# Self-attention: the value products of a unit's four chunks gathered into one visit of TensorE

## The reference, cut to what matters

```python
q = (x @ Wq.T + bq).reshape(b, l, h, hd).transpose(0, 2, 1, 3)   # b=16, l=64, h=32, hd=16
k = (x @ Wk.T + bk) ...
v = (x @ Wv.T + bv) ...
scores = jnp.einsum('bhqd,bhkd->bhqk', q, k) / math.sqrt(hd)
scores = jnp.where(causal, scores, -jnp.inf)
att = jax.nn.softmax(scores, axis=-1)
out = jnp.einsum('bhqk,bhkd->bhqd', att, v)                        # the value products
return out.transpose(0, 2, 1, 3).reshape(b, l, d) @ Wo.T + bo
```

## Time and profile before

| | us |
|---|---|
| median of three runs | 704.95 |
| the profiled execution, whole | 706.06 |
| its span, first to last instruction | 704.2 |
| TensorE busy in the span | 694.8 |
| the 110 us from 538.5 to 648.5 (the 16 steps): TensorE busy | 110.0 |
| the same: VectorE busy | 95.0 |
| the same: GpSimd busy | 89.7 |
| the same: ScalarE busy | 74.9 |

### The profile page before, as it was taken

One profiled execution on the slowest core, in us unless ns is written; L12 is line 12 of the kernel. 1 busy time (PEld: TensorE's weight loads), 2 busy tenths in 40 slices (PEclk: granted clock), 3 DMA queues, 4 the chain that ended last, 5 costly groups with the idle time before them and its releaser, 6 DMA issues.

```text
span 704.2 us, 12879 instructions
## 1 busy us (share of the span) xinstructions
PE 694.8 (99%) x4841; PEld 564.0 (80%) x4841; DVE 516.4 (73%) x815; ACT 373.0 (53%) x560; POOL 471.6 (67%) x360
## 2 busy tenths in 40 slices
PE   8999999899999999999999999999999999999998
PEld 6887888688888888888888888887888888887886
DVE  5566988967767767857758758748668888899734
ACT  6356665634743743753653653654246777665220
POOL 2698155877777778778777877844525799985630
PEclk9999999999999999999999999999999999999999
DMA  7645613140400311310310312200300101011003
GB/s 263 221 150 176 172 46 106 75 164 17 135 31 18 132 35 38 106 45 30 104 45 30 104 45 65 87 16 2 104 2 1 46 31 33 2 47 46 16 1 119
DMA packets 25736, 51.08 MB, mean 73 GB/s; under 512 B 2400, under 2 KB 10720, under 8 KB 25696
## 3 DMA queue, kind: packets, MB, share of 16 engines
q1 hardware_dynamic: 25696, 50.53, 21.8%
HBM read 40.04 MB, written 10.49 MB: 72 GB/s over the span
## 4 chain that ended last, share of the span: by engine, by line
PE 83%; DVE 5%; POOL 4%; DMA 3%; issue 2%; ACT 2%; SPq 1%; DVEq 0%; POOLq 0%; ACTq 0%
PE pj L1625 12%; PE pv L1712 10%; PE pj L1712 10%; PE pj L1816 9%; PE tp L1625 8%; PE sc L1681 4%; PE tp L1712 4%; PE pj L2000 3%; PE pv L1611 3%; PE sc L1866 2%; PE tp L1879 2%; PE pv L1890 2%; PE pv L1699 2%; PE tp L1688 2%; PE sc L1699 2%
## 5 line engine op out<-in xcount | busy, mean ns | idle before, releaser
L496 POOL TENSOR_TENSOR sw<-sw,cst 128x512 f32<-128x512 f32 x72 | 96.9, 1345 | 42.3 <-ACT sw L681 42.0
L520 POOL TENSOR_TENSOR sm<-sm,mx 128x512 f32<-128x512 f32 x64 | 73.0, 1147 | 29.6 <-DVE mx L1234 16.0
L525 POOL TENSOR_TENSOR sm<-sm,rz 128x512 f32<-128x512 f32 x64 | 70.7, 1120 | 27.0 <-DVE rz L1249 27.0
L502 POOL TENSOR_TENSOR qr<-t,sw 128x512 f32<-128x512 f32 x54 | 73.9, 1369 | 7.7
L1625 PE MATMUL tp<-x,w 128*128 128x512 f32 x288 | 74.5, 395 | 0.0
L805 ACT ACTIVATE sm<-sm 128x512 f32<-128x512 f32 x64 | 40.1, 633 | 53.4 <-POOL sm L520 53.1
L514 POOL TENSOR_TENSOR w<-raw,w 128x896 fp32r<-128x896 f32 x24 | 50.3, 2118 | 26.0 <-ACT w L658 26.0
L1816 PE MATMUL pj<-xh,ws 128*128 128x512 f32 x192 | 64.6, 402 | 0.2 <-ACT kb L899 0.2
L1625 PEld LDWEIGHTS tp<-x,w 128*128 128x128 f32 x288 | 53.0, 188 | 10.8
L658 ACT ACTIVATE w<-raw 128x1792 fp32r<-128x1792 f32 x15 | 25.6, 1705 | 59.7 <-DVE raw L1109 59.7
L1625 PE MATMUL pj<-xt,w 128*128 128x512 f32 x192 | 51.7, 407 | 0.0
(11 more groups left out here) (279 smaller groups left out, 1849.6 us busy)
## 6 DMA issues: line engine op xcount, KB each, us to landing
rawd<-in_w_d SPq DMA_DIRECT2D x16, 512.0 KB, 3.4
raw<-in_w_q SPq DMA_DIRECT2D x15, 512.0 KB, 3.3
kscr<-sm SPq DMA_DIRECT2D x16, 256.0 KB, 2.1
vscr<-sm SPq DMA_DIRECT2D x16, 256.0 KB, 2.6
kr<-kscr SPq DMA_DIRECT2D x8, 512.0 KB, 3.2
vv<-vscr SPq DMA_DIRECT2D x16, 256.0 KB, 3.5
raw<-in_w_v SPq DMA_DIRECT2D x4, 512.0 KB, 3.9
X<-in_x SPq DMA_DIRECT2D x4, 512.0 KB, 6.8
```

Of the source, the lines that this page charges most:

```text
L496: pool.tensor_tensor(bs(sw[par][:, :]), bs(sw[par][:, :]), rep(cst[:, C_SIN:C_SIN + S], HB), ALU.mult).then_inc(sin_done, 1)
L502: pool.tensor_tensor(o, bs(t1[par][:, :]), bs(sw[par][:, :]), ALU.add).then_inc(rope, 1)
L520: pool.tensor_tensor(s3, s3, per_group(mx[:, c, :], 8), ALU.subtract).then_inc(subbed, 1)
L525: pool.tensor_tensor(s3, s3, per_group(rz[:, c, :], 8), ALU.mult).then_inc(normed, 1)
```

## The change

Two things move, and two buffers are added. TensorE does no value products in first steps; in second steps it does those of all four chunks of the unit, one after the other. VectorE does no `select_out` in first steps and four in second steps, in the place where two stood. `pts` has four buffers in place of two, and the four results of a unit lie in the two `pv` banks, two chunks to a bank. The waits follow: a unit's first value product waits until the unit before is selected, and the first `select_out` waits for all four value products. ScalarE's `pt_copy` gets a further wait, for the value products of the unit before.

```diff
-        pts = [sb(ss, f"pts{i}", [P, 512]) for i in range(2)]
+        pts = [sb(ss, f"pts{i}", [P, 512]) for i in range(SCH)]
...
+        def spv_cols(n):
+            return pv[:, n % 2, n % SCH // 2 * 256:n % SCH // 2 * 256 + 256]
...
             def pt_copy(n):
                 act.wait_ge(pt_t, n + 1)
-                act.activation(pts[n % 2][:, :], tp[:, n % 2, :], ACT.Copy).then_inc(pt_done, 1)
+                if n >= SCH:
+                    act.wait_ge(spv, n // SCH * SCH)
+                act.activation(pts[n % SCH][:, :], tp[:, n % 2, :], ACT.Copy).then_inc(pt_done, 1)
...
             def select_out(n):
                 v, c = n // SCH, n % SCH
                 t, h = UNITS[v]
-                src = pv[:, n % 2, 0:256].rearrange("p (b r q) -> p b r q", b=2, r=2)
-                dve.wait_ge(spv, n + 1)
+                src = spv_cols(n).rearrange("p (b r q) -> p b r q", b=2, r=2)
+
+                dve.wait_ge(spv, n // SCH * SCH + SCH)
...
-                for n in pair:
-                    select_out(n)
+                if c == 2:
+                    for n in range(2 * m - 2, 2 * m + 2):
+                        select_out(n)
...
                 h = v % 2
                 pe.wait_ge(pt_done, n + 1)
-                if n >= 2:
-                    pe.wait_ge(ssel, n - 1)
+                if c == 0 and v:
+                    pe.wait_ge(ssel, n)
                 for b in range(2):
                     for t in range(2):
-                        last = pe.matmul(pv[64 * t:64 * t + 64, n % 2, b * P:(b + 1) * P],
+                        last = pe.matmul(spv_cols(n)[64 * t:64 * t + 64, b * P:(b + 1) * P],
                                          vc[h][:, 2 * c + b, t, :],
-                                         pts[n % 2][:, (2 * t + b) * P:(2 * t + b + 1) * P], start=True, stop=True)
+                                         pts[n % SCH][:, (2 * t + b) * P:(2 * t + b + 1) * P], start=True, stop=True)
...
-                pv_s(n)
-                pv_s(n + 1)
+                if c == 2:
+                    for i in range(n - 2, n + 2):
+                        pv_s(i)
```

## The result

The changed kernel took 714.96 us as the median of six runs (713.36 to 716.32), the kernel before 705.58 (704.57 to 706.62): a ratio of 1.0132, 95% interval 1.0109 to 1.0154, that is 9.3 us more (7.7 to 10.9). I had forecast 8.6 more. The profiled execution of the changed kernel is the quickest of the six, 713.36 us with a span of 711.4, against 706.06 and 704.2 before.

The account below looks back on a forecast made before the run. TensorE was taken to bound the kernel before, the loop through VectorE and GpSimd after. Delays of 6.99 by unit 6, 0.88 and 0.7 gave 8.6 us on 704.95: 713.6 us, range 707 to 716.5.

Parts of the forecast that it names:

- the walk: Unit-by-unit reckoning of TensorE's delay at the transposes of second steps' second tiles: 0.18 us in unit 0, 6.99 in unit 6.
- the sum: Whole delay: 6.99 us by unit 6, 0.88 for the last joined visit, 0.7 at the output projection: 8.6 us.
- The loop: From one second step's mask through VectorE, GpSimd and ScalarE to the next: 15.03 or 16.12 us against TensorE's 14.72.
- short side job: GpSimd's work between normalising and the next subtraction: a pass takes 15.03 us with a short one, 16.12 with a long one.
- Gaps: TensorE's small gaps at value visits: joining two visits saves 0.15 us a unit, 1.2 us in all (0 to 1.5).
- Unit 0: Its opening transposes already come when their tile is ready, so the removed visit's 1.03 us turn into a wait.
- the end: Output projection waits for the last unit's low part: selections 1.40 us later against TensorE, less 0.71 of room: + 0.7.
- The waits: TensorE's transposes wait for GpSimd's normalised tile at eight second-step openings: some 9 us, 2.75 of it in unit 6.
- The first: Rival: only TensorE's saved gaps count, 1.2 us less, 703.8 us; chance 0.12.
- The second: Rival: longer path to the normalised tile, but masks always follow their scores and delay does not grow: 4.6 us, 709.5; chance 0.20.
- The third: Rival: waits lower TensorE's clock, one 7.2 us step at 1.2 instead of 2.4 GHz: 720.8 us; chance 0.06.
- the path behind the selections: From a second step's mask through selections, sums and GpSimd's normalising to the second tile: 8.50 us against TensorE's 8.31.

Follow-up runs that it names:

- Experiment 2: Changed kernel with GpSimd's three long side jobs (units 2, 4, 5) moved behind the subtraction of the same step: 711.88 us, ratio 1.0089 to the kernel before.
- experiment 1: Changed kernel with TensorE's value products put back pair by pair, four selections staying in second steps: 712.75 us, ratio 1.0104 to the kernel before.
- experiments 3: Changed kernel with two selections in the second step, two behind the sums of the next unit's first step: 708.05 us, ratio 1.0036 to the kernel before.
- experiment 6: Changed kernel with joined visits in units 1 to 4 only and split selections there, the rest pair by pair: 704.97 us, ratio 0.9995 to the kernel before.

## Why the prediction was right

**The result.** 9.3 us more by the ratio (7.7 to 10.9), 8.6 forecast. The median of 714.96 is 1.4 above the forecast time of 713.6; 0.6 of that is the kernel before, which came out at 705.58 this time. In the profiled executions the stage can be measured from its first scores. The kernel before, then the changed one:

```profile
541.52 1.10 PE L1866 MATMUL sc<-kb,qm 64*64 64x128 f32 x32
```

```profile
540.17 1.10 PE L1874 MATMUL sc<-kb,qm 64*64 64x128 f32 x32
...
652.65 1.97 PE L1898 MATMUL pv<-pts,vc 128*64 128x128 f32 x32
...
659.66 0.50 PE L2008 MATMUL pj<-woh,al 128*128 128x512 f32 x1 [0.51 <-POOL al L591]
```

To the last value visit: 652.65 - 540.17 = 112.48 against 647.06 - 541.52 = 105.54, 6.94 more; the walk said 6.99. To the product that waits for the last low part: 119.49 against 652.52 - 541.52 = 111.00, 8.49 more; the sum said 8.6. From that product to the end of the span both take 51.7 us, so what lies behind passes the delay on, as forecast. What the medians have beyond 8.5 us no trace shows.

The walk holds on the way too. The transposes of the second tile in unit 6's second step start at 635.76. Before, that tile was due at 631.52, and the stage began 1.35 us later. So its delay is 635.76 + 1.35 - 631.52 = 5.59 us; the walk said 5.59.

**The loop, by its passes.** Masks of second steps in the changed kernel start at 548.71, 563.86, 579.97, 594.97, 611.09 and 627.20, so the passes take 15.15, 16.11, 15.00, 16.12 and 16.11 us. Forecast were 15.03 with a short side job (the first and third) and 16.12 with a long one. Experiment 2 shows that the side job counts, and experiment 1 that the selections on VectorE alone do it.

**Gaps.** 0.15 us a unit was forecast, a choice between 0 and 0.19; visits show 0.17, and units 0.13 in experiments 3 and 6. That it came so close is partly luck, and the sum hardly depends on it: once the loop sets the pace the saving turns into waiting, and the figure enters only in the last visit.

**Unit 0 and the end.** In unit 0 the freed 1.03 us turned into a wait (0.53 and 0.34 us shown before its two tiles, 0.87 together). The waits are a little shorter than forecast: 2.4 against 2.75 in unit 6, 7.1 in all against some 9 (the weight loads' 10.6 lie above it). At the end the product began at 659.66, where it could have at 658.99 (658.76 and one product of 0.23): 0.67 us of waiting, 0.7 forecast.

**Rivals.** The first, that only the gaps count, is what experiment 6 is for four units, with 0.5 us where 0.15 a unit makes 0.6. The second, the longer path without the feedback, would have given 709.5 and no effect of experiment 2. The third, a lower clock for a whole step, is not in the trace: the granted clock of the profiled execution is 1.00 throughout, with weight loads waiting up to 2.3 us at a time. Two of the other five executions had a mean of 0.998, and they are the longest, 716.31 and 716.32 us. Where their clock fell, and how much of their 3 us over the profiled one is due to it, is not shown.

**What I had wrong.** Not in the forecast, but in what I made of it next: I held the path behind the selections for the whole matter, and expected all four behind the sums to be free of cost. VectorE's order has two places where it waits for other engines, and I had moved its cover from one to the other. The forecast's own path was right, but it was not the only one.

## What to carry to other kernels

Before gathering small pieces of work on the engine that bounds, follow the engine that empties its results: gathered there too, they stand in one lump between two operations of a chain. Add up the closed path, from one operation through all engines back to the same operation a unit later, and compare it with the bounding engine's unit; here 13.6 to 14.7 us against 14.9 without the lump, and 15.0 to 16.1 with it. Work that nothing waits for soon is best put where its engine waits for others. Here two pieces in each of two such places cost 2.5 us, four in either one 9.3 or 7.8.

## What the runs showed of the hardware

A joined value visit (32 records of products) lasts 0.17 us less than two single ones, and a unit with it 0.13 us less. In the profiled execution TensorE kept its full granted clock (2.4 GHz) through waits of 2.1 to 2.3 us in a stage with short waits in every unit; two of the five unprofiled ones had a mean of 0.998. And four VectorE operations, 1.4 us, moved from one place in the list to another made a pass 16.11 or 15.00 us long in place of 14.87, with a long or a short side job on GpSimd; split over two places they left TensorE's regular units without a wait.
